# Graph attention and a mixture of experts on one core: the value products of every second 1024-column chunk as three fp16 products, split by GpSimd

## The reference

```python
def gnn(x, adj, Wq, Wk, Wv, weightr, weightd, bias):     # N = 4096, D = 128, 2 heads of 64
    q, k, v = ((x @ W).reshape(N, 2, 64) for W in (Wq, Wk, Wv))
    scores = einsum('nhd,mhd->hnm', q * 64 ** -0.5, k)
    attn = softmax(where(adj > 0, scores, -9e15), axis=-1)     # adj: 4096 x 4096, int32, 0 or 1
    sat = einsum('hnm,mhd->nhd', attn, v).reshape(N, 128)
    out = concatenate([sat[:2048] @ weightr, sat[2048:] @ weightd]) + bias
    return leaky_relu(out, 0.01)

x = x + gnn(layernorm(x), ...)
x = x + ffn(layernorm(x), ...)   # 8 experts of 256, the 2 highest gates chosen, gelu; all experts are computed
```

## Time and profile before

| | |
|---|---|
| median of 3 runs | 859.27 us (857.78 to 860.64) |
| the profiled execution | 858.09 us, its span 856.1 us, mean TensorE clock 0.992 |
| PE / PEld busy | 812.1 us (95%) / 596.3 us (70%) |
| DVE busy | 624.6 us (73%) |
| ACT busy | 678.9 us (79%) |
| POOL busy | 221.3 us (26%) |
| L892 `attend`, PE | 251.6 us, 4096 records of 276 ns, overlapping |
| L861 `scores`, PE | 190.0 us, 1536 records |
| L876 `transposes`, PE | 182.9 us, 4096 records |
| L406 exp, ACT | 292.8 us, 256 of 1144 ns |
| L577 masking, DVE | 312.0 us, 256 of 1220 ns |

### The profile page before, as it was taken

One profiled execution on the slowest core, in us unless ns is written; L12 is line 12 of the kernel. 1 busy time (PEld: TensorE's weight loads), 2 busy tenths in 40 slices (PEclk: granted clock), 3 DMA queues, 4 the chain that ended last, 5 costly groups with the idle time before them and its releaser, 6 DMA issues.

```text
span 856.1 us, 31746 instructions
## 1 busy us (share of the span) xinstructions
PE 812.1 (95%) x12080; PEld 596.3 (70%) x12080; DVE 624.6 (73%) x1506; ACT 678.9 (79%) x1099; POOL 221.3 (26%) x233
## 2 busy tenths in 40 slices
PE   4969999999999999999999999999987889999997
PEld 1627777777777777777777777777765656666675
DVE  6587888888888888888888888888883374444444
ACT  3838887878788787887878788787877678998985
POOL 4180000100100000010000001000000778878785
PEclk9989999999999999999999999999999899999999
DMA  8515533443343344334334433433100000000000
GB/s 219 108 22 91 82 58 58 66 75 55 58 77 55 55 70 71 55 60 75 55 55 74 67 55 62 73 55 57 29 0 2 2 14 14 14 13 12 12 12 12
DMA packets 40900, 44.96 MB, mean 53 GB/s; under 512 B 22168, under 2 KB 32160, under 8 KB 40864
## 3 DMA queue, kind: packets, MB, share of 16 engines
q0 software_dynamic: 9216, 33.56, 24.7%
q1 hardware_dynamic: 31216, 10.71, 5.4%
q10 hardware_dynamic: 432, 0.20, 0.1%
HBM read 71.72 MB, written 2.10 MB: 86 GB/s over the span
## 4 chain that ended last, share of the span: by engine, by line
PE 72%; POOL 17%; issue 6%; DVE 3%; DMA 1%; POOLq 1%; DVEq 0%; ACT 0%
PE ps L892 28%; PE ps L861 19%; PE ps L876 19%; POOL prob L337 17%; PE ps L903 2%; DVE prob L577 1%; PE ps L817 1%; PE ps L822 1%; PE ps L830 1%; PE ps L911 1%; PE ps L808 1%; DMA x_sb<-in_x 1%; POOLq L336 0%; DVE stats L501 0%; DVE mask L545 0%
## 5 line engine op out<-in xcount | busy, mean ns | idle before, releaser
L577 DVE CUSTOM_DVE_ANT_0 prob<-ps,mask 128x1024 f32<-128x1024 f32 x256 | 312.0, 1220 | 90.4 <-PE ps L861 84.6
L406 ACT ACTIVATE prob<-prob,nmax 128x1024 f32<-128x1024 f32 x256 | 292.8, 1144 | 9.9 <-DVE nmax L585 9.9
L892 PE MATMUL ps<-pt,v_sb 128*64 128x128 f32 x4096 | 251.6, 276 | 0.0
L892 PEld LDWEIGHTS ps<-pt,v_sb 128*64 128x64 f32 x4096 | 221.0, 137 | 13.4 <-issue 7.5
L421 ACT ACTIVATE pt<-ps 128x1024 f32<-128x1024 f32 x128 | 131.1, 1024 | 112.6 <-PE ps L876 112.6
L876 PEld LDWEIGHTS ps<-ident,prob 64*128 64x128 f32 x4096 | 151.9, 139 | 79.4 <-issue 79.3
L861 PE MATMUL ps<-k_half,q_row 64*128 64x512 f16 x1536 | 190.0, 380 | 4.8 <-DVE low L577 4.8
L876 PE MATMUL ps<-ident,prob 64*128 64x64 f32 x4096 | 182.9, 228 | 10.3 <-DVE pt L595 5.7
L337 POOL TENSOR_TENSOR prob<-prob 128x512 f16<-128x512 f32 x128 | 148.2, 1160 | 38.5 <-ACT prob L471 33.6
L282 POOL DMA_DIRECT2D mask<-in_adj x64 | 35.5, 554 | 429.4 <-DVE low L577 429.4
L772 DVE SCALAR_TENSOR_TENSOR x_sb<-ps,k_half,x_sb 128x128 f32 (+1 forms) x256 | 72.1, 344 | 99.5 <-PE ps L1008 99.2
(11 more groups left out here) (96 smaller groups left out, 657.7 us busy)
## 6 DMA issues: line engine op xcount, KB each, us to landing
mask<-in_adj POOLq DMA_DIRECT2D x64, 512.0 KB, 5.6
q_row<-q_nat SPq DMA_DIRECT2D x128, 32.0 KB, 4.8
x_sb<-in_x SPq DMA_DIRECT2D x4, 512.0 KB, 7.0
out<-x_sb SPq DMA_DIRECT2D x8, 256.0 KB, 2.3
pt<-in_L_ffn_W SPq DMA_DIRECT2D x1, 1024.0 KB, 6.5
wq_sb<-in_L_gnn_Wq ACTq DMA_DIRECT2D x1, 64.0 KB, 2.9
wk_sb<-in_L_gnn_Wk ACTq DMA_DIRECT2D x1, 64.0 KB, 4.5
wv_sb<-in_L_gnn_Wv ACTq DMA_DIRECT2D x1, 64.0 KB, 5.6
```

Source lines behind the costliest of these rows:

```text
L406: act.activation(prob[:, h, cols], prob[:, h, cols], ACT.Exp, bias=nmax[:, h:h + 1], scale=-1.0, accum_out=sums[:, j, h, p:p + 1]).then_in ...
L577: dve.tensor_tensor_reduce(out=prob[:, h, col_of(p)], in0=ps[:, 2 * (u % 2):2 * (u % 2) + 2, :].rearrange("p b c -> p (b c)"), in1=mask[:, ...
L892: ins = pe.matmul(ps[dims, AV, 0:P], v_sb[:, tile, dims], pt[:, UNITS.index((h, p)), t, :], start=(tile == 0), stop=(tile == NT - 1))
```

## The change

Chunks 1 and 3 (the odd units' chunks) are multiplied with the values as three fp16 products: high values times high probabilities, high values times low probabilities, low values times high probabilities. Chunks 0 and 2 stay fp32.
- **ScalarE** copies every odd unit whole into a ring of two, `pt_raw`; of the even units 0 and 4 it copies one bank and VectorE the other (`DVE_UNITS = (0, 4)`), of 2 and 6 both.
- **GpSimd** gets a `step` of its own: for each odd unit `split_pt` makes `pt_hi` (a conversion to fp16) and `pt_lo` (a subtraction); the two halves of the adjacency load and the small power stand between the splits. The values of chunks 1 and 3 are split once, after step 0. The value weights are scaled by 32 (and `wrd` by 1/32) by GpSimd. The FFN's weight splits move from before the loads of tile 2 to behind step 1's splits; their raw weights load to `x2t_hi` and `x2t_lo`.
- **TensorE**: `project_v` moves from the prologue into step 0, two chunks per quarter; the transposed x stays whole, in the place of `pt`. `AV_BLOCK` is 2: `attend` of chunks 2 and 3 of tile i-2 in the first two quarters, of chunks 0 and 1 of tile i-1 after. `x2_transpose` and `logits` move from the third and fourth quarter of an even step to the first and second of the next odd step, `out_project` from the second to the third quarter.
- **VectorE**: a masking of an odd unit waits for that unit's transposes (before, the copy ahead of it did). `x2t_low` moves to u = 1 and `keep_logits` to u = 3 of the odd step, `normalise` to u = 7 of the even step, `finish_tile` to u = 3, `divide` to u = 5, `leaky` and `residual` to u = 7 of the odd step.

```diff
-AV_BLOCK = 1
+AV_BLOCK = 2
+DVE_UNITS = (0, 4)
+V_UP = 2.0 ** 5
+            def split_pt(j, u, early=False):
+                q, p = u // 2, UNITS[u][1]
+                pool.wait_ge(pt_by_act, NU * j + u + 1)
+                if not early:
+                    pool.wait_ge(av_done, NP * j + p - 3)
+                pool.nop(nofuse=True)
+                pool.tensor_scalar(pt_hi[:, q, :, :], pt_raw[:, q % 2, :, :], 1.0, 0.0, ALU.mult,
+                                   ALU.add).then_inc(pt_hi_by_pool, 1)
+                pool.wait_ge(pt_hi_by_pool, NU // 2 * j + q + 1)
+                pool.tensor_tensor(pt_lo[:, q, :, :], pt_raw[:, q % 2, :, :], pt_hi[:, q, :, :],
+                                   ALU.subtract).then_inc(pt_by_pool, 1)
...
@@ GpSimd @@
+            def step(i, par, early=False, load=True, post=True):
+                split_pt(i - 1, 1, early)
+                split_pt(i - 1, 3, early)
+                if load:
+                    load_adj_half(i + 2, par, 0)
+                if post and par == 0:
+                    inverse_std(i - 4)
+                split_pt(i - 1, 5, early)
+                split_pt(i - 1, 7, early)
+                if load:
+                    load_adj_half(i + 2, par, 1)
...
@@ ScalarE, copy_pt @@
                 if u % 2:
+                    if not (early and u < 4):
+                        act.wait_ge(pt_by_pool, NU // 2 * j + u // 2 - 1)
+                    to = pt_raw[:, u // 2 % 2, :, :]
...
@@ VectorE, step @@
                 for u in range(NU):
-                    if prior and u % 2:
+                    if prior and u in DVE_UNITS:
                         copy_pt(i - 1, u, early)
                     if now:
-                        mask_scores(i, par, u)
+                        mask_scores(i, par, u, prior)
                         if u in (5, 7):
                             row_max(i, u // 7, u)
-                    if u == 1 and finish:
+                    if post and par == 1 and u == 1 and ready:
+                        x2t_low(i - 5)
+                    if post and par == 1 and u == 3 and ready:
+                        keep_logits(i - 5)
+                    if u == 3 and finish:
                         finish_tile(i - 2, par)
                     if ahead and u in (3, 7):
                         make_mask(i + 1, 1 - par, u // 4)
                     if post and par == 1:
                         if u == 1:
                             invert_sums(i - 3)
-                        if u == 3:
+                        if u == 5:
                             divide(i - 3)
-                        if u == 5:
+                        if u == 7:
                             leaky(i - 3)
-                        if u == 7:
                             residual(i - 3)
...
@@ TensorE, attend @@
                 for t in range(KT):
                     first, final = p == 0 and t == 0, p == NP - 1 and t == KT - 1
+                    if p % 2:
+                        for values, probs, end in ((0, pt_hi, False), (0, pt_lo, False), (1, pt_hi, final)):
+                            for h in range(HEADS):
+                                dims = slice(h * DH, (h + 1) * DH)
+                                ins = pe.matmul(ps[dims, AV, 0:P], v_pair[:, values, p // 2, t, dims],
+                                                probs[:, UNITS.index((h, p)) // 2, t, :], start=False, stop=end)
+                    else:
...
@@ TensorE, prologue @@
-                project_v(2 * p)
-                project_v(2 * p + 1)
```

More of the change, by code:

```diff
@@ L312, in _ @@
             pool.tensor_scalar(ident16[:, :], ident[:, :], 1.0, 0.0, ALU.mult, ALU.add).then_inc(w_split_chain, 1)
[L314 to L329, removed]
+            pool.tensor_scalar(wrd[:, :, :, :], wrd[:, :, :, :], 1.0 / V_UP, 0.0, ALU.mult, ALU.add).then_inc(w_split_chain, 1)
+            step(2, 0, post=False)
+            step(3, 1)
+            pairs(pool, 4, NT - 2, step)
+            step(NT - 2, 0, load=False)
+            step(NT - 1, 1, load=False)
+            step(NT, 0, load=False)
+            inverse_std(NT - PAIR)
             def ffn(j, par):
@@ L398, in _ @@
                     normalise_x(2 * p + 5)
+            for j in range(NC):
+                copy_v(j)
             def exp_unit(j, u):
@@ L435, in step @@
                         copy_pt(i - 1, u, early)
-                    if post and u == 5:
-                        x2t_high(i - 4)
+                    if post and u == 2:
+                        x2t_high(i - 5)
                     if u < NU - EXP_LEAD and prior:
@@ L448, in _ @@
             step(3)
-            pairs(act, 4, NT, lambda i, par: step(i, post=par == 0))
-            step(NT, now=False, post=True, last=True)
+            step(4)
+            step(5, post=True)
+            pairs(act, 6, NT, lambda i, par: step(i, post=par == 1))
+            step(NT, now=False, last=True)
+            x2t_high(NT - 2 * PAIR)
             act.wait_ge(b1_in, 16)
@@ L732, in _ @@
             step(2, 0, post=False)
-            step(3, 1)
-            pairs(dve, 4, NT - 2, step)
+            step(3, 1, ready=False)
+            step(4, 0)
+            step(5, 1)
+            pairs(dve, 6, NT - 2, step)
             step(NT - 2, 0)
@@ L739, in _ @@
             choose_gates(0, 0, RANKED_EARLY)
+            x2t_low(NT - 2 * PAIR)
             finish_tile(NT - 1, 1)
             invert_sums(NT - PAIR)
+            keep_logits(NT - 2 * PAIR)
             divide(NT - PAIR, bank=PREP0 + 1)
@@ L923, in logits, with step @@
                 ins.then_inc(logit_psum, PAIR)
-            def step(i, par, prior=True, now=True, drain=True, post=True, early=False):
+            def step(i, par, prior=True, now=True, drain=True, post=True, ready=True, early=False):
                 for k in range(NU // 2):
@@ L951, in _ @@
             pe.wait_ge(w_split_chain, W_SPLITS)
-            step(3, 1)
-            pairs(pe, 4, NT, step)
+            step(3, 1, ready=False)
+            step(4, 0)
+            step(5, 1)
+            pairs(pe, 6, NT, step)
             step(NT, 0, now=False)
-            for p in range(NP - AV_BLOCK, NP):
-                attend(NT - 1, p)
+            attend(NT - 1, NP - 2)
+            x2_transpose(NT - 2 * PAIR)
+            attend(NT - 1, NP - 1)
             def gate_transpose(j):
```

143 lines of the change are left out of this document (88 added, 55 removed).

## The result

The changed kernel takes 1055.83 us (median of four, 1051.86 to 1057.07), the kernel before 858.52 beside it: ratio 1.2288, 95% interval 1.2264 to 1.2313. The forecast was 963 in a range of 880 to 995: the direction is right, the size is 93 us short, and the time lies outside the range.

A forecast was written before the change was run, and what follows sets the result against it. Attention was taken as TensorE's before; afterwards T1 and T5 wait for VectorE's copies, delayed by GpSimd. Profiled 858.1 + 75 (pairs) + 16 (statistics) + 7 (start) + 3 (step 3) + 4 (end) = 963 us, range 880 to 995.

The forecast's parts named there:

- walk: Interval-by-interval sum over a pair of attention steps: 42.75 us against 37.36, +5.4 a pair, +75 over fourteen pairs.
- the lock: In attention, VectorE's make_mask, leaky and residual wait for whichever GpSimd instruction is in the way; without it, 37.05 a pair.
- The rival without it: No lock in attention, only the reordered queues: 37.05 us a pair, 865 us in all; chance 12%.
- the two turns: T7 to the next T1: 4.98 us into an odd step (4.2 without the lock), 7.5 into an even (4.5).
- the masking stretch of the odd step: T3 to T5 of the odd step: late maskings, make_mask meeting the subtraction; 6.85 us, 5.3 without the lock.
- Conversion 1.04 and subtraction 2.13: GpSimd's two instructions over 128x1024 per odd unit, in us; with semaphores 3.3, four times a step 13.2.
- the fp16 block: TensorE's value block of 48 fp16 products, two per step: 1.45 us taken, between 1.33 and 2.65; fp32 1.90.
- 0.64 + 1.90 + 1.87 = 4.41: TensorE's T1 to T3 in the even step with an fp32 value block, in us.
- normalise (0.34, reads one tensor) I take as free: VectorE's normalise in attention does not wait for GpSimd's instructions and stays at 0.34 us.
- the statistics' two-column instruction (+16): VectorE's tensor_scalar in the even step, if shut out by unit 1's subtraction: 2.25 us a pair, 31; half taken.
- Start and step 3: Weight splits in GpSimd's queue ahead of step 2's splits delay T0 of step 3, +7 us; step 3 itself +2.7.
- the end: Last value block waits for GpSimd, plus the moved x2_transpose and the ranking ahead of copy 0: +4 us.

The follow-up runs named there:

- the first experiment: The changed kernel with GpSimd's conversion and subtraction cut to 2 of 1024 columns, queues, order and semaphores kept; 874.6 us.
- The third experiment: The changed kernel with 34 spare fp16 products of 224 columns on TensorE ahead of unit 1's transposes; 1022.5 us.
- the sixth experiment: The changed kernel with ScalarE making all copies, leaky at unit 6, residual at 1, normalise at 4, GpSimd's rsqrt between two splits; 898.2 us.
- experiments 6 and 7: The sixth experiment (898.2 us), then the same kernel with each GpSimd conversion and subtraction in two pieces of 512 columns (919.2 us).
- the eighth experiment: The kernel before with value products of chunks 1 and 3 as two fp16 products, probabilities rounded, nothing new for GpSimd; 816.0 us.

## Why the prediction fell short

Its walk gave a pair of 42.75 us; this one took 51.09, and the 14 pairs 49.9 in the mean. Interval by interval, from the timeline of the pair at 474 to 526 us (Tn, the transposes of unit n):

| interval | walk | measured | off |
|---|---|---|---|
| even step, T1 to T3 | 4.41 | 7.17 | +2.76, clock |
| T3 to T5 | 4.35 | 4.25 | |
| T5 to T7 | 4.41 | 4.42 | |
| T7 to T1, into the odd step | 4.98 | 6.79 | +1.81, normalise |
| odd step, T1 to T3 | 4.78 | 6.36 | +1.58, clock |
| T3 to T5 | 6.85 | 6.96 | |
| T5 to T7 | 5.47 | 7.10 | +1.63, clock |
| T7 to T1, into the even step | 7.5 | 8.03 | +0.53 |

- **Right: the lock as the cause, and its place.** The rival without it is what the first experiment built (874.6 for its 865), and the two turns and the masking stretch of the odd step, where the walk put the blocked make_mask, leaky and the subtraction, agree within 0.6 us apart from normalise.
- **Right: the costs of single instructions.** Conversion 1.04 and subtraction 2.13 where nothing meets them, and the fp16 block: in the changed kernel it starts at 488.08 and the next transposes at 489.54, 1.46 for the 1.45 taken.
- **Failed, the largest: every TensorE interval was taken at full speed ("0.64 + 1.90 + 1.87 = 4.41").** The kernel before has no idle stretch in mid attention and so no row at the lower clock there; but the prediction itself put waits of 1 to 5 us into each pair and did not ask what the clock does behind them. Three intervals are 5.97 us longer for it in this pair, and 70 us (33, 16 and 21) over the 14 pairs, of the 93 that are missing. The third experiment filled the waits before two of these and took their 48 us away. The third interval, behind T5 in the odd step, with 2.91 and 1.81 us for the value block and out_project in place of 1.97 and 1.13, was not filled; there the windows view shows the granted clock itself, 0.59 from 516.9 to 518.6 us and 0.65 from 518.6 to 521.5.
- **Failed: "normalise (0.34, reads one tensor) I take as free".** 1.81 a pair, 25 us in 14. It is a tensor_scalar within SBUF like make_mask, and I had cited such a one as blocked (1022 ns in the earlier trace rows) two sentences before. Reading one tensor was the wrong test: it takes 2143 ns at its longest and 333 at its shortest.
- **Half taken, not there: the statistics' two-column instruction (+16).** In this kernel it falls into the last 0.12 us of a conversion in 14 of 16 cases and is not lengthened (170 ns). But where a subtraction begins just ahead of it, it is shut out (2.10 us in 14 of 16 cases of the sixth experiment), so the doubt was about its place in time.
- **Start and step 3 +11.4, not +10; the end +10.9, not +4.** At the end the copy of unit 0 in the last step stands behind leaky's and residual's last work and the whole ranking of the experts: its T1 follows T0 by 9.58 us where it was 1.88. The walk had this wait, and sized it too small.
- By these terms the forecast would have been 963 - 16 + 70 + 25 = 1042; the turns into the even steps add 6, the start 1 and the end 7, and that is the 1056 measured.

The range failed with the clock: every bound in it was of VectorE's and GpSimd's side. Without the clock's 70 us the time would have been some 986 and inside it.

## What to carry to other kernels

Before giving GpSimd elementwise work beside a busy VectorE, list every tensor_scalar within SBUF and every two-input instruction that VectorE has between two results TensorE waits for: each can cost a whole GpSimd instruction and more, however small it is (here 170 ns became 2100, and 426 became 2337), and moving them one by one moves the lock (experiments 6 and 7). When a walk through the waits gives TensorE idle stretches like those of this kernel (1.96 to 3.78 us; behind 0.19 to 0.46 us the value blocks kept their 1.97), count with a lower clock for what follows (0.50 to 0.68 over the value blocks looked at): here it cost 0.9 to 1.7 us for each value block behind one, at unit 1 of the odd step in ten of fourteen cases, at the other two places each time. And ask first whether the work for GpSimd is needed at all: here the two products of the eighth experiment need none, and are 240 us faster than the three.

## What the runs showed that I had not expected

- A two-column tensor_scalar of 170 ns takes 2100 when a GpSimd subtraction of 2.1 us begins just ahead of it.
- Between GpSimd instructions that follow each other make_mask mostly got its turn, and two fp32 tensor_scalars, normalise and ve, did not.
- Behind a wait of 2.5 us the granted clock was 0.50 in ten of fourteen odd steps and 1.00 in four, with the same work on both sides.
- GpSimd's memsets, which only write, lengthen make_mask, a tensor_scalar (686 to 1184 ns in the median), and not leaky, with two inputs (406).
- 64-column fp16 weights of two heads side by side: 48 products in 1.46 us, 30 ns each, and 32 weight loads in 0.92, 29 each.
- The lock works on GpSimd too: the subtraction, 2.12 to 2.17 in 82 cases of 128 without make_mask in at its start, takes 2.43 to 2.46 in the 45 with it.
